# Layer 1's experts: four of eight token chunks routed to their two experts instead of computed for all eight

## The reference, cut to what matters

```python
gates = softmax(xf @ gW + gb)                    # 8 experts
top2_scores, top2_idx = top_k(gates, 2)
w = (one_hot(top2_idx, 8) * top2_scores[..., None]).sum(1)
h = relu(einsum('nd,edf->enf', xf, W1) + b1)     # d = 128, f = 256
y = einsum('enf,efd->end', h, W2) + b2
out = einsum('ne,end->nd', w, y)                 # then x1 + out, a layer norm, the gate, and onto x
```

## Time and profile before

| | us |
|---|---|
| median of 3 runs | 2780.31 |
| lowest, highest | 2777.49, 2783.54 |
| the profiled execution | 2766.23 |
| its span, on which all rows are measured | 2764.4 |
| busy: TensorE, VectorE, ScalarE, GpSimd | 2608.0, 2017.9, 1665.9, 1183.3 |
| one value product of layer 1's experts, first and last start | 1760.9, 2011.2 |

### The profile page before, as it was taken

One profiled execution on the slowest core, in us unless ns is written; L12 is line 12 of the kernel. 1 busy time (PEld: TensorE's weight loads), 2 busy tenths in 40 slices (PEclk: granted clock), 3 DMA queues, 4 the chain that ended last, 5 costly groups with the idle time before them and its releaser, 6 DMA issues.

```text
span 2764.4 us, 67999 instructions
## 1 busy us (share of the span) xinstructions
PE 2608.0 (94%) x24870; PEld 1786.7 (65%) x24870; DVE 2017.9 (73%) x5620; ACT 1665.9 (60%) x4107; POOL 1183.3 (43%) x1620
## 2 busy tenths in 40 slices
PE   6999999998999999999997999999989989999898
PEld 2666666666687666666664555677767755666676
DVE  6988888876644666676666998466678885887675
ACT  3888888885335766777764777443335544334665
POOL 6888888863602565111124454122333321014441
PEclk9999999999999999999999999999999999999999
DMA  3022221212374111121115543000054433435750
GB/s 114 17 54 76 77 75 48 68 33 82 131 230 129 37 41 42 32 48 32 24 25 145 164 135 122 1 14 3 29 162 140 126 92 63 93 79 158 205 166 28
DMA packets 218857, 230.81 MB, mean 83 GB/s; under 512 B 18608, under 2 KB 188272, under 8 KB 216480
## 3 DMA queue, kind: packets, MB, share of 16 engines
q1 hardware_dynamic: 212000, 207.58, 27.2%
q10 hardware_dynamic: 3456, 12.58, 1.4%
q0 software_dynamic: 3072, 6.30, 0.8%
HBM read 165.87 MB, written 75.60 MB: 87 GB/s over the span
## 4 chain that ended last, share of the span: by engine, by line
PE 73%; DVE 12%; ACT 7%; issue 4%; POOL 2%; DMA 1%; SPq 1%; ACTq 0%; DVEq 0%; POOLq 0%
PE pb L163 65%; ACT big L967 4%; PE pb L663 3%; ACT big L160 2%; DVE big L3014 2%; DVE big L837 2%; PE pb L596 2%; DVE big L236 1%; DVE big L3519 1%; PE pb L2985 1%; PE pb L249 1%; DVE big L820 1%; DVE big L747 1%; POOL hs L1853 1%; DVE big L842 0%
## 5 line engine op out<-in xcount | busy, mean ns | idle before, releaser
L163 PE MATMUL pb<-big 128*128 128x128 f32 (+12 forms) x19624 | 2345.0, 327 | 94.2 <-ACT big L160 32.4
L163 PEld LDWEIGHTS pb<-big 64*128 64x128 bf16 (+4 forms) x19624 | 1476.5, 143 | 750.8 <-issue 422.6
L160 ACT ACTIVATE big<-pb 128x512 f32<-128x512 f32 (+7 forms) x1481 | 846.3, 620 | 541.0 <-PE pb L163 293.0
L160 ACT ACTIVATE big<-pb,big 128x512 f32<-128x512 f32 (+2 forms) x502 | 276.6, 586 | 406.7 <-PE pb L163 356.1
L3014 DVE TENSOR_REDUCE big<-pb 128x4 f32<-128x1024 f32 (+1 forms) x256 | 277.6, 1086 | 71.4 <-PE pb L163 66.8
L967 ACT ACTIVATE big<-big 128x256 f32<-128x256 f32 x512 | 254.0, 499 | 69.5 <-DVE big L842 68.2
L967 ACT ACTIVATE big<-pb,big 128x128 f32<-128x128 f32 (+1 forms) x512 | 257.1, 527 | 60.3 <-DVE big L822 60.1
L837 DVE CUSTOM_DVE_ANT_0 big<-pb,big 128x256 f32<-128x256 f32 x512 | 186.7, 422 | 96.9 <-PE pb L163 96.7
L187 POOL TENSOR_SCALAR big<-big 128x4 f32<-128x4 f32 (+2 forms) x102 | 26.8, 263 | 533.7 <-DVE big L182 533.6
L174 POOL TENSOR_TENSOR big<-big 128x128 f32<-128x128 f32 x168 | 74.8, 459 | 340.8 <-DVE big L171 340.7
L1046 POOL TENSOR_TENSOR big<-big 128x512 f32<-128x512 f32 x128 | 159.9, 1277 | 141.6 <-DMA big<-recip 141.5
(11 more groups left out here) (211 smaller groups left out, 2454.0 us busy)
## 6 DMA issues: line engine op xcount, KB each, us to landing
parts<-big SPq DMA_DIRECT2D x384, 96.0 KB, 2.4
big<-parts SPq DMA_DIRECT2D x72, 512.0 KB, 4.1
big<-recip SPq DMA_DIRECT2D x128, 256.0 KB, 4.9
big<-comb SPq DMA_DIRECT2D x32, 512.0 KB, 8.2
hs<-in_zero SPq DMA_DIRECT2D x10, 1472.0 KB, 8.7
big<-in_wx SPq DMA_DIRECT2D x31, 450.0 KB, 4.4
parts<-big SPq DMA_DIRECT2D x192, 64.0 KB, 2.1
big<-parts ACTq DMA_DIRECT2D x24, 512.0 KB, 4.7
```

The costliest lines, as they stand in the source:

```text
L160: return e.activation(o, i, f, bias=bias, scale=scale)
L163: return e.matmul(o, l, r_, start=start, stop=stop, skip_group_check=True)
```

## The change

Layer 1's experts become a stage of their own, `routed_ffn()`, of T = 16 + 23 + 16 = 55 steps. Chunks 0 and 1 are dense (16 units), chunks 2 to 5 are routed (2048 tokens with two choices each, in 23 blocks of 256 rows), chunks 6 and 7 are dense (16 units).

- The x1 rows get a 129th column. The row buffer `hs1` (18432 rows of 129 words) is written by 32 indirect DMAs of 128 rows; the 129th word of a row is the row of a result buffer `ys1` into which its result belongs. VectorE writes that column for the tokens' first choices, GpSimd overwrites it for the second choices, after the DMAs before have landed.
- Of a block, SP loads 256 rows (6 buffers) and the weights of the expert (4 buffers of 642 columns). TensorE makes 2 transposes, 2 ups of 256 columns and 4 downs, ScalarE the ReLU, VectorE adds the bias and copies the block's 129th words. GpSimd writes the two halves of the result with two indirect DMAs to `ys1`, by token (4 buffers).
- `ys1` is then read in plain order, two results for each token. Chunks 2 and 3 are combined in steps 43/44 and 47/48 of the stage, chunks 4 and 5 in steps 20/21 and 36/37 of layer 2's attention, where SP fetches them at b = 4. For each: VectorE sums and makes the statistics, GpSimd the reciprocal roots, ScalarE normalizes, GpSimd scales, shifts, gates and adds onto X.
- The first pieces of the stage take 11 steps of layer 1's attention instead of 9. x1 is added with the seed, by VectorE. Layer 2's attention does its statistics at i = 5 and 6 instead of 2 and 4, and SP's second gates are at b = 11 instead of 5.
- `hs1` is filled beforehand: nine more copies of 1.06 MB in layer 0's attention, which give every unused row an own row in the unread part of `ys1`.
- Several stages now share one semaphore for VectorE's own waits and one for GpSimd's.

```diff
-            own, own_g = moe_own
+            own, own_g = vector_own, gpsimd_own
@@ layer 0's attention, SP
+                    if causal and 2 <= b < 11:
+                        part = slice(2064 * (b - 2), 2064 * (b - 1))
+                        e.dma_start(dr["hs1"]...[:, part], dr["blank"][:, part]).then_inc(st_zero, 16)
@@ routed_ffn
+            hosted = {0: [(0, "x1")], 1: [(2, "turn")], 2: [(0, "logits")], 3: [(0, "gate")], 4: [(2, "logits")], 5: [(3, "turn")],
+                      6: [(0, "spread")], 7: [(3, "logits")], 8: [(0, "seed")], 9: [(2, "max")], 10: [(3, "max")]}
+            beside = {0: [("A", "index"), ("A", "route"), (1, "x1")], 1: [("A", "rank"), (1, "logits"), (4, "turn")], 2: [(4, "logits"), (4, "max")],
+                      3: [(1, "gate"), (5, "turn")], 4: [(5, "logits"), (5, "max")], 5: [("B", "route")], 6: [("B", "rank"), (1, "spread")],
+                      7: [(1, "seed")], 8: [("B", "table_a")], 9: [("B", "table_b")], 10: [("B", "table_c")], 13: [("B", "exp")], 14: [("B", "share")],
+                      18: [(6, "x1")], 19: [(6, "logits")], 21: [(6, "gate")], 22: [(7, "x1")], 24: [(6, "spread"), (7, "logits")],
+                      26: [(6, "seed")], 27: [(7, "gate")], 30: [(7, "spread")], 32: [(7, "seed")]}
+            three = ("g", 0), ("g", 1), ("y", 0)
+            scatters = {t: [(m, three[m % 3]) for m in range(3 * (t - first), min(3 * (t - first) + 3, 16))]
+                        for first in (2, 8) for t in range(first, first + 6)}
+            combined_at = {T1 + 4: 0, T1 + 8: 1}
...
+            def tensor(e):
+                for t in range(T + 2):
+                    if dense_n(t) >= 0 and t < T:
+                        tensor_up(e, dense_n(t))
+                    elif t < T:
+                        tensor_block_up(e, t - T0)
+                    if T0 <= t + 1 < T1:
+                        tensor_rows(e, t + 1 - T0)
+                    for n in downs(t):
+                        tensor_down(e, n)
+                    if T0 < t <= T1:
+                        tensor_block_down(e, t - 1 - T0)
+                    for q, p in beside.get(t, []):
+                        tensor_piece(e, q, p)
...
+            def vector_block_down(e, j):
+                y, J = slots["y", T0 + j], NBLK + j
+                bk = empty(e, y)
+                if j >= 4:
+                    e.wait_ge(y_placed[j % 4], 32 * (j // 4))
+                e.tensor_copy(SPOT[j % 4], RB[j % 6][:, :, 128])
+                e.tensor_tensor(YB[j % 4], bk[:, 0:256]..., WB[J % 4][:, 514:642]..., ALU.add).then_inc(y.free, 1)
...
+            def gpsimd_scatter(e, m):
+                g, h, k, t = m // 16, m % 16 // 4 // 2 % 2, m % 16 // 4 % 2, m % 4
+                n = 8 * g + 4 * h + t
+                if m % 16 == 0:
+                    e.wait_ge(placed, 3 + g + 1)
+                if m % 8 == 4:
+                    e.wait_ge(scattered, 16 * (48 + m))
+                    e.tensor_copy(X1[:, 8 + n:12 + n, 128], INDEX[1][:, n:n + 4]).then_inc(own_g.sem, own_g.up())
+                    e.wait_ge(own_g.sem, own_g.n)
+                at = PLACE[g][:, 8 * k + 4 * h + t:8 * k + 4 * h + t + 1]
+                e.indirect_dma_start(out=dr["hs1"], out_offset=bass.IndirectOffsetOnAxis(ap=at, axis=0),
+                                     in_=X1[:, 8 + n, :], in_offset=None).then_inc(scattered, 16)
+            def gpsimd_block_out(e, j):
+                y = slots["y", T0 + j]
+                e.wait_ge(y.free, y.n)
+                for i in range(2):
+                    e.indirect_dma_start(out=dr["ys1"], out_offset=bass.IndirectOffsetOnAxis(ap=SPOT[j % 4][:, i:i + 1], axis=0),
+                                         in_=YB[j % 4][:, i, :], in_offset=None).then_inc(y_placed[j % 4], 16)
+            def gpsimd(e):
+                for t in range(T + 2):
+                    if tail_at(t - 1) >= 0:
+                        tail.gpsimd(e, tail_at(t - 1))
+                    for m, (key, f) in scatters.get(t, []):
+                        s = slots["y", t - 2] if key == "y" else slots["g", t, f]
+                        e.wait_ge(s.full, s.n)
+                        gpsimd_scatter(e, m + (16 if t >= 8 else 0))
+                    if T0 < t <= T1:
+                        gpsimd_block_out(e, t - 1 - T0)
...
+            def sync_weights(e, j):
+                if j >= 4:
+                    y = slots["y", T0 + j - 4]
+                    e.wait_ge(y.free, y.n)
...
+            def sync(e):
+                tail.sync(e)
+                e.wait_ge(table_made, 2)
+                for j in range(4):
+                    sync_weights(e, j)
+                e.wait_ge(scattered, 16 * (48 + 32))
+                for j in range(6):
+                    sync_rows(e, j)
+                for j in range(NB1):
+                    if j + 4 < NB1:
+                        sync_weights(e, j + 4)
+                    if j + 6 < NB1:
+                        sync_rows(e, j + 6)
...
+                for m in range(6):
+                    late_ffn_fetch(e, m)
+                guest.sync(e)
@@ layer 2's attention
+            def late_at(t):
+                return [(c, p) for c, first in ((2, 20), (3, 36)) for p, at in (("sum", 0), ("norm", 1)) if causal and first + at == t]
@@ VectorE, after rowmax(e, t) and the posts of t - 1
+                        for c, p in late_at(t - 1):
+                            if p == "sum":
+                                late_ffn_vector(e, c)
@@ ScalarE, after the exponential and the posts of t; GpSimd, after the steps and posts of t
+                    for c, p in late_at(t):
+                        if p == "norm":
+                            late_ffn_scalar(e, c)
@@ SP
-                    if k == 2 and b == 5:
-                        e.wait_ge(gated, 8 + 32 * (k - 1))
+                    if k == 2 and b == 11:
+                        e.wait_ge(ffn_added, 8)
+                        e.wait_ge(gated, 24)
                         second_gates(e, k)
```

More of the change, by code:

```diff
@@ L141, in program @@
         ld_emb = sem("ld_emb")
-        ld_x = [sem(f"ld_x{k}") for k in range(8)]
+        ld_rows = [sem(f"ld_rows{k}") for k in range(8)]
         ld_wa, ld_wf, ld_wm, ld_wi, ld_tri = (sem(f"ld_{n}") for n in ("wa", "wf", "wm", "wi", "tri"))
@@ L3238, in gpsimd @@
                         gpsimd_post(e, step, b)
+                    for c, p in late_at(t):
+                        if p == "norm":
+                            late_ffn_gpsimd(e, c)
                     if 0 <= t - guests_at < guest.steps:
```

680 lines of the change are left out of this document (651 added, 29 removed).

## The result

The changed kernel takes 2794.6 us (median of 5, 2790.2 to 2795.23) against 2779.12 (5, 2772.49 to 2783.54): ratio 1.006 [1.0044, 1.0075], 15 us slower. Forecast was 2751, 29 us faster. Measured twice more, the ratio was 1.0049 [1.003, 1.0069] and 1.0009 [0.9997, 1.0022]. So most of the 15 us comes with the occasion of the measurement, and apart from it the forecast gain is gone.

A forecast was written before the change was run, and what follows sets the result against it. TensorE was taken as the bound, busy throughout layer 1's experts and 98% in layer 2's attention. Experts' stage -49 and combining +20 gave -29 us, from the median 2780.3 to 2751 us, range 2724 to 2772.

The forecast's parts named there:

- The sum for the experts' stage: Layer 1's experts: new stage 198.2 us against 249.2, -51, with +1.8 at the end of layer 1's attention: -49 us.
- The combining: Chunks 4 and 5 in layer 2's attention: VectorE, GpSimd and ScalarE in order delay TensorE 10 us, twice: +20 us.
- Rival (b): Layer 2's attention: the combining hides, since TensorE works eight steps behind the maxima; +4 instead of +20, 2735 us; chance 0.20.
- The dense chunks that go: Layer 1's experts: a dense chunk is 28.0 us of units and 3.07 of gate pieces; stage before 249.2 us, 32 units remain.
- The scatter: Before layer 1's blocks: GpSimd's queue lasts to about 72 us, TensorE begins the blocks at 75.6 after waiting 16 us.
- Rival (a): Before layer 1's blocks: the scatter is ready by unit 15 or nearly; 9 to 16 us of wait go, 2739 us; chance 0.10.
- The blocks: Layer 1's 23 routed blocks: period 2.55 us, between 2.0 and 3.4; 62 us for the section.
- fall largely into TensorE's gaps: Layer 1's blocks: pieces of chunks 6 and 7 (6.1 us), modulation (1.5) and two last dense downs (3.5) fill TensorE's idle time.
- The weights' loop: Layer 1's blocks: four buffers, the load for block j+4 waits for block j's result; bounds the period at 2.55 us.
- GpSimd's 2.53: Layer 1's blocks: two indirect DMAs a block, 0.96 us each and 0.31 of issue before each, bound the period at 2.53 us.
- What costs nothing: Row buffer fills in layer 0's attention, and tables, indices and sums of chunks 2 and 3 in dense units, hide: 0 us.
- The hosted pieces: End of layer 1's attention: two turns and two sets of logits more, taken whole: +1.8 us.
- Rival (d): Layer 1's blocks: GpSimd's indirect DMAs slow to 2.2 us each beside VectorE, period 4.4, +42 us, 2793 us; chance 0.05.

The follow-up runs named there:

- after_third: The changed kernel, unchanged, measured a third time against the kernel before: 2769.27 us against 2766.24, ratio 1.0009.
- after_again: The changed kernel, unchanged, measured once more beside the kernel before: 2793.22 us against 2781.07.

## Why the prediction was wrong

Two steps of the prediction failed. The sum for the experts' stage, -49 us, took too much off for the units that go and too little for the blocks and the last units; and the move of the statistics in layer 2's attention had no price at all. By traces of one kind (after_third and the kernel before) the change is +2.8 us; forecast was -29. The 31.8 us between them are made up of the terms below. They add up to 36. The start of the blocks gives 2 back (counted from the first value result it moved 14 to 15 us against the kernel before, where the sum had 16.4), and 2 or 3 lie in the rounding and where one section ends and the next begins.

- **An edit that had no price: +9.** The move of the statistics to steps 5 and 6 stands in the change, and the prediction doesn't mention it. It costs 10 to 13 us, alone (10.8 us by the traces) as in company; 9 is what the attention's +29.1 leaves beside the forecast 20. Without it the change is a small gain (0.9975), with it none.
- **The combining: +20 forecast, 19.7 measured.** Mechanism and place as forecast: waits on VectorE and on ScalarE at two places 44 us apart. Rival (b), that it hides, is out. Its parts were off, so that the sum came out this close is in part luck. TensorE waited 5.12 us for the exponential where I had 7.6, and 1.66 us for the maximum where I had nothing; the 2 us for the negated maxima didn't come. In their place stands the clock, which the sum had left out here: in the trace after, TensorE works 5 us at a granted 0.50 behind each combining, which loses some 2.5 us.
- **The dense chunks that go: 10 us too many.** My sum took the whole stage at 249.2 us and the last 16 units at 56. But it put all seven chunks' pieces into the other 48 units, and the last 16 host pieces, a gate and a guest as well: in the kernel before their first and last value results start 60.4 us apart (1949.95 and 2010.38), not 52.5. Four chunks are 4 x 31.07 = 124.3 us; the sum had taken off 249.2 - 59.2 - 56 = 134.
- **The scatter: right.** The first block was forecast at 75.6 us from the stage's first ups, and it came 77.1 us after (1769.27 to 1846.36; 76.8 in after_third). TensorE waited 6.3 us there and not 16, because it was late itself: 6.30 us for VectorE, and half the clock behind that (granted 0.50 from 1830 to 1835). Rival (a) had a wait gone for want of a late scatter; here the wait shrank and the start stayed.
- **The blocks: 66.6 forecast (2 + 1.75 + 62 + 0.85), 74.1 measured, 80 to 85 with the unnamed waits.** That the pieces "fall largely into TensorE's gaps" failed. There are hardly any gaps to fill: bare blocks come 2.33 us apart, not because the matmuls take longer than the 2.0 of my sum, but because the ups wait for ScalarE's ReLU and copy, a ring that I hadn't priced. 23 x 2.33, 11.1 of pieces and 3.3 of a wait for a gate are 68.0; the rest of the 74.1 is half clock (0.96 granted, an estimated 3 us) and small waits. The weights' loop, one of my two bounds, is none. GpSimd's 2.53 is more than the bare 2.33, and it issues without a pause for the 22 us before 1904, but the blocks come 3.02 apart on average, and VectorE never waits for a landing there; with SP's stores it is 72.5, less than 2 us under the 74.1. By the rule of the Trainium skill, DMA: Bandwidth & Descriptors, section How a descriptor splits into AXI transactions, I had estimated that loads of 129-word rows cost up to half again. On a fifth of the bytes that would be some 11% more share per byte, by the same estimate; 0.60 at 165 GB/s, against 0.86 at 240, is 1 to 2% more, so the trace doesn't show it.
- **"What costs nothing" failed once.** The three-way chain of a combining in the last units does hold something: not a ReLU, but the roots of the next norm behind it. The last units take 77.3 us from the blocks' end, against 72.5 for the same units before, and the attention's first maximum starts 4.2 us behind the last value result instead of 1.3: 5 + 3 us. The fills cost nothing, as forecast (layer 0's first block at 758.49 against 761.55).
- **The hosted pieces: +3.8**, not +1.8, from the attention's last maximum to the first value result (31.2 against 27.4).

Rival (d), slower by GpSimd's indirect DMAs, is the one that the measured 2794.6 looks like. It isn't what happened. They keep their 0.962 us. The slower time is the terms above, +3 us, plus the unnamed waits of some occasions: with them the kernel before takes 13 us more (2779.1 against 2766.2) and the changed one 25 (2794.6 against 2769.3). They lie where GpSimd's scatters are; their cause stays open. The forecast had nothing for them, and it had nothing to see them by.

## What to carry to other kernels

Walk the diff line by line and give every moved step a price, an innocent one too: a ring of split, stores and loads can be without any slack, and here one piece of GpSimd moved to the step before the split cost 10 us of a 280 us stage. When a stage loses units, take off what the trace shows between the same unit of two chunks, and read the last units separately. Work that three engines hand to each other belongs in as many steps as it has hands: the same operations over seven steps instead of two cost some 7 instead of 20 us. And look for rings of two engines inside a unit before you call the sum of one engine's instructions its period.

## What the runs showed of the hardware

On some occasions ScalarE, VectorE and GpSimd wait 2 to 7 us at a time with no releaser in the trace, and the kernel before takes 2776 to 2779 instead of 2766 to 2767 us. They lie where GpSimd issues indirect DMAs one behind the other: between 700 and 760 us in every kernel of such an occasion (22 us of ScalarE's and VectorE's time), and between 1800 and 1935 us where layer 1 is routed (24 to 44 us in six traces). With SP's plain stores those in the blocks went, in the one trace that there is. Timelines of after_again, the three engines at one of the places:

```profile
755.47 1.13 DVE L1689 SCALAR_TENSOR_TENSOR big<-pb,big 128x128 f32<-128x128 f32 x4 [4.97 <-remote]
755.51 1.27 ACT L160 ACTIVATE big<-pb,big 128x512 f32<-128x512 f32 x2 [7.29 <-remote]
755.71 0.95 POOL L1863 DMA_INDIRECT hs<-big  x1 [2.47 <-remote]
```

They end together, and each of them starts there on something that a matmul releases. TensorE's own records go on through these waits, from 744.50 to 754.56. So it may be TensorE's work or its signal that is late; the trace, in which the ends of matmuls are modelled, doesn't show it. The same kernel showed them on one occasion and not on another, and the kernel before took 2776.22 and 2767.05 us on two occasions on one chip. What they are stays open, and no kernel here was made to tell it. The Trainium skill, SBUF — State Buffer, section SBUF: two separate sides, says that VectorE's two-port operations keep GpSimd from writing the descriptors of its DMAs; here the other engines wait while GpSimd's DMAs keep their 0.96 us, so the rule doesn't cover it. It also means that two traces taken on different occasions can differ by 15 us for no reason of the kernel (the spans of the kernel before: 2764.4 and 2779.3).
